# A decoder layer with attention, a state-space branch and a router: its state scans cut in two halves, and its semaphore scheme rebuilt around an unchanged order

## What is computed

```python
# per batch row b of 4: x[b] is 512 tokens x 512, ctx[b] is 512 x 256
xn = layernorm(x) * g_norm
q, k, v = heads(xn @ Wq), xn @ Wk, xn @ Wv      # 16 query heads of 128, one k and one v
q, k = l2norm(q) * 4, l2norm(k) * 4
x1 = x + layernorm(concat(softmax(q @ k.T) @ v) @ Wout) * g_out
u = silu(conv4(in_proj(ctx)));  dt, B, C = x_proj(u)
delta = softplus(dt_proj(dt) + dt_b)
# 512 channels x 16 states, first order recurrence over 512 tokens:
state[n] = state[n] * exp(delta * A[n]) + delta * u * B[n];  y += state[n] * C[n]
x2 = x1 + (y + D * u) * silu(layernorm(x1)).T
# then a router over 32 experts (top 8, threshold) and the gated expert MLPs on layernorm(x2)
```

## Time and profile before

| | us |
|---|---|
| median of 3 runs (1702.66 to 1727.33) | 1707.53 |
| the profiled execution | 1710.76 |
| its span, first to last instruction | 1709.0 |
| PE busy in the span | 1429.0 |
| DVE busy | 1108.4 |
| ACT busy | 940.7 |
| POOL busy | 505.1 |

### The profile page before, as it was taken

One profiled execution on the slowest core, in us unless ns is written; L12 is line 12 of the kernel. 1 busy time (PEld: TensorE's weight loads), 2 busy tenths in 40 slices (PEclk: granted clock), 3 DMA queues, 4 the chain that ended last, 5 costly groups with the idle time before them and its releaser, 6 DMA issues.

```text
span 1709.0 us, 25100 instructions
## 1 busy us (share of the span) xinstructions
PE 1429.0 (84%) x6762; PEld 1014.4 (59%) x6763; DVE 1108.4 (65%) x1483; ACT 940.7 (55%) x2428; POOL 505.1 (30%) x367
## 2 busy tenths in 40 slices
PE   4899988979988898898979889988943746999996
PEld 1577664447766554676755367766432635777774
DVE  5354887665588874657986565689664424666663
ACT  4676773357567345665834567575320424666652
POOL 0000010000017420000762000048403554766664
PEclk9799999989999998999989989999965978999998
DMA  7695587334469643364876227367911557899985
GB/s 245 258 272 153 138 216 168 77 100 112 127 151 225 173 106 100 59 176 124 200 190 139 74 70 198 92 145 174 272 49 20 129 109 174 215 237 237 239 196 69
DMA packets 137430, 265.38 MB, mean 155 GB/s; under 512 B 45945, under 2 KB 47434, under 8 KB 128513
## 3 DMA queue, kind: packets, MB, share of 16 engines
q0 software_dynamic: 36480, 126.75, 33.2%
q1 hardware_dynamic: 75120, 86.70, 17.9%
q10 hardware_dynamic: 25744, 50.87, 9.4%
HBM read 170.57 MB, written 46.21 MB: 127 GB/s over the span
## 4 chain that ended last, share of the span: by engine, by line
PE 31%; DMA 24%; DVE 15%; ACT 13%; issue 9%; POOL 5%; SPq 3%; POOLq 1%; ACTq 0%; DVEq 0%
DMA out<-y_ring,add_ids 11%; PE bank L756 8%; DMA y<-dbu 6%; PE bank L628 4%; POOL lists L1922 4%; DMA y<-state 3%; PE bank L646 3%; DVE dbu L1511 3%; PE pair L580 2%; ACT q_s L1017 2%; PE pair L582 2%; PE pair L581 2%; ACT decay L1052 2%; PE bank L504 2%; ACT junk L1006 1%
## 5 line engine op out<-in xcount | busy, mean ns | idle before, releaser
L646 PE MATMUL bank<-v_aug,probs 128*128 128x129 f32 x2048 | 248.1, 279 | 8.5 <-ACT probs L1046 8.5
L646 PEld LDWEIGHTS bank<-v_aug,probs 128*128 128x128 f32 x2048 | 239.6, 194 | 17.4 <-ACT probs L1046 16.4
L1922 POOL DMA_INDIRECT lists<-entry,slot x128 | 215.8, 1686 | 103.4 <-DVE slot L1695 64.3
L756 PE MATMUL bank<-wout,o_t 128*128 128x512 f32 x512 | 237.3, 618 | 0.7 <-DMA wout<-in_wout 0.7
L1046 ACT ACTIVATE probs<-bank 128x512 f32<-128x512 f32 x256 | 145.9, 606 | 108.5 <-PE bank L628 93.2
L1052 ACT ACTIVATE decay<-delta,neg_a 128x511 f32<-128x511 f32 x256 | 164.8, 736 | 64.3 <-DVE dbu L1511 31.4
L756 PEld LDWEIGHTS bank<-wout,o_t 128*128 128x128 f32 x512 | 99.9, 199 | 124.5 <-issue 124.0
L1937 POOL DMA_DIRECT2D y<-dbu x32 | 29.5, 922 | 467.6 <-DVE dbu L1516 455.9
L1511 DVE TENSOR_TENSOR_SCAN state<-decay,state 128x2048 f32<-128x2048 f32 x32 | 141.6, 4424 | 26.0 <-ACT decay L1052 24.9
L1982 POOL DMA_INDIRECT out<-y_ring,add_ids x68 | 127.0, 1868 | 92.2 <-DMA out<-y_ring,add_ids 65.0
L1511 DVE TENSOR_TENSOR_SCAN dbu<-decay,dbu 128x2048 f32<-128x2048 f32 x32 | 141.4, 4420 | 9.9 <-ACT decay L1052 9.8
(11 more groups left out here) (231 smaller groups left out, 2949.6 us busy)
## 6 DMA issues: line engine op xcount, KB each, us to landing
y<-dbu POOLq DMA_DIRECT2D x32, 1024.0 KB, 9.6
wq<-wq_dram POOLq DMA_DIRECT2D x30, 1024.0 KB, 11.1
y<-state POOLq DMA_DIRECT2D x28, 1024.0 KB, 9.3
w_raw<-in_w_exp ACTq DMA_DIRECT2D x32, 768.0 KB
wout<-in_wout SPq DMA_DIRECT2D x64, 256.0 KB, 4.9
b_bc<-bc_dram SPq DMA_DIRECT2D x64, 256.0 KB, 3.8
c_bc<-bc_dram SPq DMA_DIRECT2D x64, 256.0 KB, 4.8
w_raw<-in_w_exp ACTq DMA_DIRECT2D x32, 512.0 KB
```

What stands on the lines that cost most here:

```text
L646: mm = pe.matmul(bank_o[half][:, (t % 2) * (DH + 1):(t % 2 + 1) * (DH + 1)], probs[:, k, t * P:(t + 1) * P], v_aug[:, k, :], start=(k == 0 ...
L756: mm = pe.matmul((bank_o + bank_s)[t][:], o_t[:, h, t * P:(t + 1) * P], wout[:, h % 4, :], start=(h == 0), stop=(h == H - 1))
L1922: pool.indirect_dma_start(out=lists, out_offset=bass.IndirectOffsetOnAxis(ap=slot[:, t, k:k + 1].bitcast(U32), axis=0), in_=entry[:, t, :] ...
```

## The change

The order of the instructions is the same on all five engines, with one exception: each of the 64 scans of 2048 columns is now two of 1024, one for the channel blocks 0 and 1, one for 2 and 3. What else changes is which semaphores an instruction waits for.

- `state_scan(r, n, half)` waits for two decays instead of four. The decays of the first two blocks of state n+1 wait for the first half of scan n, the other two for the second half. `state_product` waits for both halves, as before.
- The query norms have two sets of scratch, used by turns (`job % 2`), and a counter of their own; the LayerNorms have another set (`ls_...`) with `ls_ln`, `ls_seed` and `nl`. Squares and seeds of a query pair now wait for the pair two before, not for the last one; DVE no longer waits at the end of a query norm.
- The first decays of a row wait for `delta_ok` rather than for the end of `skip`.
- The transposes of a row's first two heads (`q_tr`) wait for `oc_ok`, the copies of the output projection of the row before; before, only the scores behind them did.
- Helpers are cut into smaller steps, each with all the waits that it needs for itself, so that many instructions wait for something that an earlier one has already waited for. Counted in the built programs, the wait instructions that stand alone rise from 399 to 638 on ACT, 218 to 395 on DVE, 420 to 769 on PE, 147 to 178 on POOL and 36 to 99 on SP.
- The programs are written out as lists of calls (`first_row`, `row`, `last_row`) in the order that they had.

```diff
-            def state_scan(r, n):
-
-                now = place[n % 2][:].rearrange("p e t -> p (e t)")
-                dve.wait_ge(S["dA_ok"], r * DS * ET + n * ET + ET)
+            def state_scan(r, n, half):
+
+                es = slice(2 * half, 2 * half + 2)
+                now = place[n % 2][:, es, :].rearrange("p e t -> p (e t)")
+                dve.wait_ge(S["dA_ok"], r * DS * ET + n * ET + 2 * half + 2)
                 dve.wait_ge(S["dbu_ok"], r * DS + n + 1)
-                dve.tensor_tensor_scan(now, dA, now, 0.0, ALU.mult, ALU.add).then_inc(S["scan_ok"], 1)
+                dve.tensor_tensor_scan(now, dA3[:, es, :].rearrange("p e t -> p (e t)"), now, 0.0, ALU.mult, ALU.add).then_inc(S["scan_ok"], 1)
...
             def state_product(r, n):
                 i = n % 2
-                dve.wait_ge(S["scan_ok"], r * DS + n + 1)
+                dve.wait_ge(S["scan_ok"], (r * DS + n + 1) * 2)
...
             def decays(r, n):
 
-                act.wait_ge(S["scan_ok"], r * DS + n)
+                if n == 0:
+                    act.wait_ge(S["delta_ok"], r + 1)
                 for e in range(ET):
+                    if n > 0:
+                        act.wait_ge(S["scan_ok"], (r * DS + n - 1) * 2 + e // 2 + 1)
                     act.activation(dA3[:, e, 1:], delta[:, e, 1:], ACT.Exp,
                                    scale=neg_a[:, bass.ds(n, 1), e:e + 1].rearrange("p a c -> p (a c)")).then_inc(S["dA_ok"], 1)
...
-            def newton(job, dst, w=4):
-
+            def q_norm(r, name):
+
+                job, w = q_job(r, name), 4 if name == "k" else 8
+                i = job % 2
                 dve.wait_ge(S["rs_seed"], job * 3 + 3)
...
                 dve.wait_ge(S["nw"], job * 2 + 1)
-                dve.scalar_tensor_tensor(out=dst[:, 0:w], in0=rs_t[:, 0:w], scalar=1.5, in1=rs_y[:, 0:w], op0=ALU.add, op1=ALU.mult).then_inc(S["nw"], 1)
-                dve.wait_ge(S["nw"], job * 2 + 2)
+                if job > 1:
+                    dve.wait_ge(S["kn_ok" if Q_JOBS[(job - 2) % len(Q_JOBS)] == "k" else "q_ok"], reads_of(job - 2))
+                dve.scalar_tensor_tensor(out=rs_r[:, i, 0:w], in0=rs_t[:, i, 0:w], scalar=1.5, in1=rs_y[:, i, 0:w], op0=ALU.add, op1=ALU.mult).then_inc(S["nw"], 1)
...
+            def q_seed(r, name):
...
+                if job > 1:
+                    act.wait_ge(S["nw"], (job - 1) * 2)
...
+            def q_tr(r, g, i):
+
+                pe.wait_ge(S["q_ok"], r * H * 4 + g * 16 + 16)
+                if i >= 2:
+                    pe.wait_ge(S["qT_ok"], r * H + g * 4 + i - 1)
+                if i < 2 and g == 0 and r > 0:
+                    pe.wait_ge(S["oc_ok"], r * TT)
```

More of the change, by code:

```diff
@@ L82, with q_job, ln_job @@
 ADDED0 = 3 * 16
[L85 to L104, removed]
+def q_job(r, name):
+    return r * len(Q_JOBS) + Q_JOBS.index(name)
+def ln_job(b, name):
+    if b < 0:
+        return 0
+    return 1 + b * len(ROW_LNS) + (LAST_LNS if b == NB - 1 else ROW_LNS).index(name)
 def constants():
@@ new lines, in scores, with values @@
+                mm.then_inc(S["s_ps"], 1)
+            def values(r, h, half):
+                pe.wait_ge(S["exp_ok"], r * H * KT + h * KT + KT)
+                if h == 0:
+                    pe.wait_ge(S["v_ok"], r * 2 + 2)
+                    pe.wait_ge(S["oc_ok"], r * TT)
+                else:
+                    pe.wait_ge(S["o_ok"], r * H * TT + (h - 1) * TT + 2 * half + 2)
+                for t in (2 * half, 2 * half + 1):
+                    for k in range(KT):
+                        mm = pe.matmul(bank_o[half][:, (t % 2) * (DH + 1):(t % 2 + 1) * (DH + 1)], probs[:, k, t * P:(t + 1) * P], v_aug[:, k, :],
+                                       start=(k == 0), stop=(k == KT - 1))
+                mm.then_inc(S["pv_ps"], 1)
@@ L1060, in next_squares, with divide @@
[L1060 to L1068 removed]
+            def divide(r, h, half):
@@ L1070, in divide @@
                 act.wait_ge(S["oT_ps"], r * H + h)
-                for t in range(TT):
-                    act.wait_ge(S["den_ok"], r * H * 2 + h * 2 + (t // 2 + 1))
-                    act.activation(o_s[:, t, :], bank_o[t // 2][:, (t % 2) * (DH + 1):(t % 2) * (DH + 1) + DH], ACT.Copy,
+                act.wait_ge(S["den_ok"], r * H * 2 + h * 2 + half + 1)
+                for t in (2 * half, 2 * half + 1):
+                    act.activation(o_s[:, t, :], bank_o[half][:, (t % 2) * (DH + 1):(t % 2) * (DH + 1) + DH], ACT.Copy,
@@ L1216, in last_group, with fill_lists @@
-            def last_group(row):
-                for h in range(12, H):
-                    if h < H - 1:
-                        exps_divide(row, h)
-                    else:
-                        divide(row, h)
-                    transposed(row, h)
-                    if h < H - 1:
-                        decays(row, h - 2)
+            def fill_lists():
+                wq_stored(act)
+                act.dma_start(lists.rearrange("(e p j) c -> p e (j c)", p=P, j=PADS),
+                              a["const"][:, C_ALL:].unsqueeze(1).to_broadcast([P, NE + 1, PADS * LIST_COLS])).then_inc(S["lists_in"], 16)
```

2504 lines of the change are left out of this document (1697 added, 807 removed).

## The result

The changed kernel takes 1721.26 us (median of 20 runs, 1713.57 to 1731.38), the kernel before 1711.53 us (20 runs). The ratio is 1.0069 with a 95% interval of [1.0044, 1.0093], some 12 us; it leaves out six of the 20 runs of the kernel before, which took over 1.5 per cent longer than its fastest, and so is larger than the ratio of the two medians. The forecast was 1700.4, on a median of 1707.5 from three runs, and its range ended at 1714. The difference is within the 2 per cent for which the forecast gave 0.92. The profiled execution of the changed kernel took 1724.01 us.

A forecast was written before the change was run, and what follows sets the result against it. No engine is busy throughout, so chains between engines, through decays and scan of state 15, set the time. Terms -3.4 + 3.4 - 3.0 - 5.1 + 1.0 = -7.1 us took 1707.5 to 1700.4, range 1687 to 1714.

The forecast's parts named there:

- Cost of a half: Each scan: a half takes 2.29 us, two 0.16 more than one whole; half of that, +0.08 a state, counted.
- Term 1: Last state of three rows: DVE starts its scan sooner and everything behind follows in series, -1.14 us each, -3.4.
- Term 2: Transposes of a row's first two heads wait for the output projection's copies, nothing covers it: 1.15 us a row, +3.4.
- Term 3: Decays of state 1: ACT is done with them 1.1 us sooner, less 0.08 for later denominators; three rows, -3.0.
- Term 4: States 5 to 11, four rows: DVE's waits removed -5.8, cut +2.2, POOL's sends -1.5; sum -5.1.
- Term 5: Added separate waits and second scratch: met waits are hidden, scratch gives nothing, some 15 places on the path; +1.0, bounds 0 and +15.
- A (adds): Serial adds take term 4's gain, as waits for decays turn into waits for adds: 1707.5 us; chance 0.17.
- B (sends): Sends that meet a scan are done after at most 2.3 us instead of 4.61, 6.3 us off: 1695.6; chance 0.08.
- C (clock): Shorter stalls of ACT bring back a quarter of PE's lost clock, 9 us in three rows: 1691; chance 0.11.
- D: Met waits in the queues of ACT and DVE are not hidden, 0.07 us each, +14.5: 1713.9; chance 0.16.

The follow-up runs named there:

- e4_split: The kernel before with the halved scans and their waits alone, without new scratch, further waits or the wait in the transposes: ratio 1.0048 to the kernel before.
- e1_table: The changed kernel without the wait for `y_ok` ahead of the four Silu of a row start: ratio 0.9992 to the kernel before.
- f3_whole_table: The changed kernel without the wait for `y_ok` ahead of the Silu, and with whole scans of 2048 columns: ratio 1.0018 to the kernel before.
- h3_whole_preload: The changed kernel with the load of Silu's table written out ahead of its waits, and with whole scans: ratio 1.0034 to the kernel before.

## Why the prediction was wrong

**What bounds the kernel.** Right that the chains between engines do, and that the pair of decays and scan was on the path in states 1 and 15. Missing was what stands next in line. I named it for the last row only.

**Cost of a half.** Right: 2.27 us for 2.29, and a pair takes 4.47, 0.05 over the whole.

**Term 1 (-3.4).** The mechanism was right as far as the scan: DVE's wait fell from 4.73 us to 3.45, and scan 15 came 1.28 sooner against ACT.

```profile
625.99 4.47 DVE L2103 TENSOR_TENSOR_SCAN state<-decay,state 128x1024 f32<-128x1024 f32 x2 [3.45 <-ACT decay L1340]
...
641.55 0.49 DVE L2021 TENSOR_SCALAR dbu<-decay,conv_w 128x512 f32<-128x512 f32 x1 [1.01 <-ACT decay L1248]
```

The step that failed is "scan, product, sum and convolution follow in series". The second pair of the convolution takes its input from ACT's copies, and these from products in PE's queue behind the output projection. They were just in time before; now DVE waits 1.01 us. Scan 15 to Silu grew by 0.94 (e4_split against before) to 1.16 us (e1_table against f3_whole_table), so of a gain of 3.9 us in states 12 to 15 of three rows some 0.8 is left. That gain is 1.3 a row, the 1.28 of scan 15, so the waits ahead of states 13 and 14 gave nothing, as I had said.

**Term 2 (+3.4).** Wait and late copy were right, a little small: 1.47 us for 1.15. "Nothing covers it" was wrong: about 1.0 us in all reached scan 0, and in the halved kernels the wait goes along with a gain behind it, as told above.

**Term 3 (-3.0).** The mechanism was right, the size in part luck: scans 0 to 4 gain 3.4 us in three rows in the means and 3.2 in the changed kernel. Of this the halves give 0.8 a row from scan 1 to 2 (33.08 to 32.28, both at a granted clock of 1.00) where I had 1.0; 0.4 a row from scan 2 to 3 (15.13 to 14.73) comes from the rest of the change, since h3_whole_preload has it too (14.76). With halves alone (e4_split) the three rows lost 1.9, with a lower granted clock in two of them. The decays of state 1 no longer wait:

```profile
713.03 2.61 ACT L1340 ACTIVATE decay<-delta,neg_a 128x511 f32<-128x511 f32 x4
```

**Term 4 (-5.1).** Wrong in sign: +3.5 in the means, within its bounds of +4.5 and -10. The failed step is "the change can remove them: -5.8". It removed them, and they came back as waits for PE and ACT, longer by PE's lower clock at state 5. With that stall taken out the term is -2.2.

**Term 5 (+1.0).** This is the mistake that counts. "A wait that is already met lies under the instruction before it" is near enough true of 490 waits on PE and ACT. I counted all of them and looked at none by its place. Three stood ahead of an activation that needs another table, where a met wait pushes an unmet one in front of the load. In the one profiled pair that is 13.2 us in three row starts; over three kernels with it and nine without (all with halves) a row start takes 82.5 against 80.4 us, 6 us in all, while the ratios of the pairs say 10 to 19 us (1.0074 to 1.0018, 1.013 to 1.0018). The bound of +15 held it, the value taken did not.

**The rivals.** A (adds): no, the inputs wait less for adds. B (sends) was right in its mechanism: of 96 sends 16 took over 3.5 us before, none does now, and POOL's busy time fell from 505.1 to 470.2 us. But the add then waits for its product, and the head for PE. The Trainium skill's rule in "SBUF — State Buffer", section "SBUF: two separate sides", is that VectorE with two SBUF inputs and a GpSimd instruction that reads SBUF keep the shared pair of ports for a whole instruction. The traces agree with it: the longest send went from 4.67 us, 0.25 over a scan, to 2.91, 0.64 over a half. C (clock) was the right quantity with the wrong sign: the granted clock went from 0.921 to 0.918, with PE idle for longer at state 5 and behind the late load. D named a time near the result (1713.9) by a mechanism that isn't there at that price: the four `o_s` still take 1.14 us. Rival A's own sum is 1707.7, not 1707.5. Two of the signs I named missed as well: sends reach 2.91 us, where I had 2.5, and DVE waits 17.1 us for decays beside the output projection, where I had at most 12.

**The sum again.** Load +6 to +13, term 1 -0.8, term 2 +1.0, term 3 -3.4, term 4 +3.5: +6 to +13 against the 12 us measured. The upper end rests on the one pair, changed kernel and e1_table, and so isn't a check of its own. The changed kernel with whole scans and the load mended stands at 1.0018 and 1.0034, 3 to 6 us over the kernel before (both intervals reach down to 1), of which term 2 is 1; what the rest is, or whether it is there, stays open, and so does which part of the load's cost lies outside the row starts.

## What to carry to other kernels

Before counting an added wait as free, look at what its engine would have done ahead of it: where a table load (or anything placed between) runs in idle time, a second wait ahead of the same instruction puts it on the path, and writing the load out ahead of the waits takes it off again. When one engine is freed sooner, ask what its successor waits for last: work done early in front of a fixed wait only lengthens that engine's idle time, and on PE this can cost more than it gave. A stall that is removed is worth what is left when the next input in line has been read from the trace, for every instruction in the series, and not only for the first.

## What the runs showed of the hardware

- A load of ACT's table takes 1.28 us and can lie wholly under a wait, with 0.01 us between it and the activation.
- PE's granted level behind an idle time is not the same in every row of one execution. Behind 2.59 to 2.83 us of idle the eight products of the x projection took over 4.9 us in 18 of 45 row starts (else 3.6), behind 3.84 to 4.02 us in 10 of 15. It fell behind 1.9 us of idle between scans 1 and 2 in some kernels and not in others. Each count is from one profiled execution a kernel, and its rows repeat each other.
- The indirect DMA issues of POOL took up to 5.17 us in the six kernels whose scans last 4.42 us (4.67 in the kernel before), and no more than 3.15 in the 14 halved ones.
- The last stage, scan 15 to the end, took 473 to 501 us in single profiled executions of kernels that don't differ there. One profile each can't place an effect of 5 us.
